# Centring the residual once a step in an AdaLN block of attention and experts

## The reference, cut to what matters

```python
h = layernorm(x) * (1 + ca) + sa
x = x + ga * attention(h)            # 16 heads of 8, window of 32 keys
h = layernorm(x) * (1 + cb) + sb     # this is xt below, 2048 tokens of 128
ew, ei = top_k(xt @ gate_w, 2)       # softmax over the two, spread to wE (experts x tokens)
hid = gelu(xt @ w1[e] + b1[e], approximate=False)        # 256 wide
o = hid @ w2[e] + b2[e]
y = layernorm(xt + o, eps=1e-6) * ln_g[e] + ln_b[e]      # for each of the 8 experts
x = x + gb * sum_e wE[e] * y[e]
```

## Time and profile before

| What | Value |
|---|---|
| Time, median of 3 runs | 253.94 us (253.59 to 254.95) |
| Profiled execution: its own time | 255.15 us |
| Profiled execution: span | 253.4 us |
| TensorE busy / weight loads / VectorE / ScalarE / GpSimd | 91% / 79% / 72% / 61% / 54% |
| Granted TensorE clock, mean | 0.978 |

### The profile page before, as it was taken

How to read it: one execution, slowest core, us unless ns; L and a number is a source line. 1 busy time by engine, 2 the same in 40 slices (tenths; PEclk the granted TensorE clock), 3 DMA queues, 4 the chain that set the end, 5 groups by cost and what they waited for, 6 DMA issues and landing times.

```text
span 253.4 us, 7792 instructions
## 1 busy us (share of the span) xinstructions
PE 230.3 (91%) x3064; PEld 200.6 (79%) x3064; DVE 182.9 (72%) x570; ACT 155.5 (61%) x419; POOL 135.8 (54%) x254
## 2 busy tenths in 40 slices
PE   7976879999899989998999899998999899989960
PEld 3753539988898889887988799888988898869950
DVE  2689957767797859785887689686968596555275
ACT  2165515966498449846695749753984589257740
POOL 8044728246752668247715674366625760378075
PEclk9998879999999999999999999999999999999996
DMA  7940000000000000000000000000000000000000
GB/s 202 360 180 0 3 2 3 0 6 0 4 21 4 3 3 20 4 3 4 0 23 3 0 3 22 5 3 3 21 3 3 3 1 23 4 0 3 21 0 22
DMA packets 5652, 6.23 MB, mean 25 GB/s; under 512 B 336, under 2 KB 5104, under 8 KB 5360
## 3 DMA queue, kind: packets, MB, share of 16 engines
q1 hardware_dynamic: 5616, 5.74, 7.0%
HBM read 4.68 MB, written 1.05 MB: 23 GB/s over the span
## 4 chain that ended last, share of the span: by engine, by line
PE 64%; DVE 25%; POOL 5%; issue 3%; DMA 1%; ACT 1%; POOLq 0%; ACTq 0%; DVEq 0%
PE z L1013 11%; DVE q_st L594 6%; PE score L984 6%; PE score L976 5%; PE turns L871 5%; PE turns L872 4%; PE turns L873 4%; DVE ypart L664 3%; PE score L995 3%; DVE xn L574 3%; PE score L1060 2%; POOL rstd L344 2%; PE turns L1081 1%; PE turns L917 1%; PE turns L1071 1%
## 5 line engine op out<-in xcount | busy, mean ns | idle before, releaser
L1013 PE MATMUL z<-w,hid 128*128 128x128 f32 x480 | 61.6, 276 | 0.0
L1013 PEld LDWEIGHTS z<-w,hid 128*128 128x128 f32 x480 | 58.8, 191 | 3.1 <-issue 1.0
L488 ACT ACTIVATE hid<-turns,pack_ffn 128x256 f32<-128x256 f32 x96 | 38.6, 517 | 32.9 <-PE turns L873 32.9
L327 POOL TENSOR_TENSOR ypart<-ypart 128x256 f32<-128x256 f32 (+1 forms) x60 | 36.1, 601 | 18.4 <-DVE ypart L664 15.4
L313 POOL TENSOR_SCALAR zvar<-zss 128x4 f32<-128x4 f32 x32 | 8.0, 249 | 62.4 <-DVE zss L650 54.4
L664 DVE SCALAR_TENSOR_TENSOR ypart<-z,zcoef,ln_gG 128x128 f32<-128x128 f32 x120 | 34.1, 340 | 1.8 <-POOL zcoef L318 1.7
L314 POOL TENSOR_TENSOR zrstd<-zvar,mhalf 128x4 f32<-128x4 f32 x32 | 32.2, 1008 | 2.7
L871 PE MATMUL turns<-h_hi,w_hi 128*128 128x256 f32 x96 | 27.8, 290 | 0.2 <-DVE h_lo L732 0.2
L872 PE MATMUL turns<-h_lo,w_hi 128*128 128x256 f32 x96 | 27.0, 281 | 0.0
L873 PE MATMUL turns<-h_hi,w_lo 128*128 128x256 f32 x96 | 27.0, 281 | 0.0
L984 PE MATMUL score<-pack_proj,prob 128*128 128x128 f32 x128 | 21.5, 292 | 2.8 <-ACT prob L449 2.8
(11 more groups left out here) (157 smaller groups left out, 517.9 us busy)
## 6 DMA issues: line engine op xcount, KB each, us to landing
w<-in_w SPq DMA_DIRECT2D x2, 1024.0 KB, 8.3
out_x<-yout SPq DMA_DIRECT2D x8, 128.0 KB, 1.8
x_tokens<-in_x SPq DMA_DIRECT2D x1, 896.0 KB, 6.9
ln_g<-in_ln_g SPq DMA_DIRECT2D x1, 512.0 KB
pack_mod<-in_pack_mod SPq DMA_DIRECT2D x1, 385.0 KB, 3.1
pack_proj<-in_pack_proj SPq DMA_DIRECT2D x1, 193.0 KB, 4.2
pack_att<-in_pack_att SPq DMA_DIRECT2D x1, 130.5 KB, 4.1
x_tokens<-in_x SPq DMA_DIRECT2D x1, 128.0 KB, 3.0
```

The costliest lines, as they stand in the source:

```text
L327: cf.link(g.tensor_tensor(ypart[:, tt, at:at + n, :], ypart[:, tt, at:at + n, :], ypart[:, tt, at + n:at + 2 * n, :], ALU.add))
L488: last = a.activation(hid[:, e, c, :], up_bank(i, e)[:, c * STEP:(c + 1) * STEP], ACT.Gelu, bias=b1[:, e, c:c + 1])
L1013: last = mm(z_bank(f, q)[:, e * D:(e + 1) * D], hid[:, ee, c, tt * P:(tt + 1) * P], w2[:, ee * CH + c, :], start=False, stop=e == HALF - 1 ...
```

## The change

Centring moves out of the quarters. `centre(i)`, new on TensorE between up(i,2) and up(i,3), multiplies h2T (fp32, 256 columns) once by a centring matrix whose last output column is zero, so that 127 channels and an empty row come out, into z1 (a score bank in the last step). `split_centred(i)`, new on VectorE between shift(n,1) and shift(n,2), reads that bank, adds a one to row 127 and splits into hc_hi and hc_lo. A quarter is then opened by two matmuls: hc_hi and hc_lo times a `spread_r` matrix that gives back 128 channels from 127 (the last is minus the sum of the others) and whose row 127 holds b2, high part in one copy and low part in the other.

centre(i) waits until scale(f,3) has read z1 (u_done, 4i). down_start(f,0) waits until the split is done (hc_s). In the first part of quarter 1, the products of its first expert move ahead of turn(i,0). On ScalarE the two constant copies (128 x 128 each) give way to one of 128 x 2048; two memsets of ones and one of 128 x 1024 go away on GpSimd; the pack of constants grows by 130 columns.

```diff
@@ scalar front
-                a.activation(ones_r[:, :], ones[:, :], ACT.Copy)
-                a.activation(center_r[:, :], center[:, :], ACT.Copy)
+                a.activation(spread_r[:, :, :, :].rearrange("p a e d -> p (a e) d"), bc(spread[:, :], 1, 2 * EXPERTS),
+                             ACT.Copy).then_inc(spread_s, 1)
@@ vector
+            def split_centred(i):
+                dve.wait_ge(hc_done, i + 1)
+                if i > 0:
+                    dve.wait_ge(z_done, 4 * i)
+                v.tensor_scalar(hc_hi[:, :], hc_bank(i)[:, 0:STEP], units[:, 0:1], None, ALU.add).then_inc(hc_hi_s, 1)
+                dve.wait_ge(hc_hi_s, i + 1)
+                v.scalar_tensor_tensor(hc_lo[:, :], hc_bank(i)[:, 0:STEP], units[:, 1:2], hc_hi[:, :].bitcast(fp32),
+                                       ALU.add, ALU.subtract).then_inc(hc_s, 1)
@@ vector body
-                    for s in range(GROUPS):
-                        shift(n, s)
+                    shift(n, 0)
+                    shift(n, 1)
+                if att:
+                    split_centred(i)
+                if nxt:
+                    shift(n, 2)
+                    shift(n, 3)
@@ tensor down_start
-                mm(by_e, h2_hi[:, f % 2, tok], bc(center_r[:, :], 1, HALF), start=True, stop=False, skip_group_check=True)
-                mm(by_e, h2_lo[:, f % 2, tok], bc(center_r[:, :], 1, HALF), start=False, stop=False, skip_group_check=True)
-                mm(by_e, ones_r[:, :], b2_rows[:, half * HALF:(half + 1) * HALF, :], start=False, stop=False,
-                   skip_group_check=True)
+                experts = slice(half * HALF, (half + 1) * HALF)
+                if q == 0:
+                    pe.wait_ge(hc_s, f + 1)
+                mm(by_e, hc_hi[:, tok], spread_r[:, 0, experts, :], start=True, stop=False, skip_group_check=True)
+                mm(by_e, hc_lo[:, tok], spread_r[:, 1, experts, :], start=False, stop=False, skip_group_check=True)
@@ tensor
+            def centre(i):
+                if i == STEPS - 1:
+                    pe.wait_ge(x1_s, i + 1)
+                elif i > 0:
+                    pe.wait_ge(u_done, 4 * i)
+                mm(hc_bank(i)[:, 0:STEP], center[:, :], h2T[:, :], start=True, stop=True).then_inc(hc_done, 1)
@@ tensor body
                     down_start(f, 1)
+                    products(f, 1, 0, 1)
...
                     up(i, 2)
+                    centre(i)
                     up(i, 3)
```

More of the change, by code:

```diff
@@ L52, in build @@
                  "mask": ((("rep", (P,)), ("masks", (2, KEYS))), P),
-                 "ffn": ((("center", (D,)), ("iota", (EXPERTS,)), ("w_gate", (EXPERTS,)), ("b1", (EXPERTS, CH))), P)}
+                 "ffn": ((("center", (D,)), ("spread", (D,)), ("units", (2,)), ("iota", (EXPERTS,)), ("w_gate", (EXPERTS,)), ("b1", (EXPERTS, CH))), P)}
         packs, part = {}, {}
@@ L69, in build @@
         rep, maskf = part["rep"], part["masks"]
-        center, iota, w_gate, b1 = part["center"], part["iota"], part["w_gate"], part["b1"]
+        center, spread, units, iota, w_gate, b1 = part["center"], part["spread"], part["units"], part["iota"], part["w_gate"], part["b1"]
         b_o = sb("b_o", [P, D])
@@ L78, in build @@
         b2_mean = sb("b2_mean", [EXPERTS, 1])
-        b2_rows = sb("b2_rows", [P, EXPERTS, D], f32r)
+        spread_r = sb("spread_r", [P, 2, EXPERTS, D], f32r)
         b2_high = sb("b2_high", [EXPERTS, D], f32r)
@@ L83, in build @@
         ln_b = sb("ln_b", [EXPERTS, D])
-        center_r = sb("center_r", [P, D], f32r)
         rep16 = sb("rep16", [P, P], bf16)
         mask16 = sb("mask16", [P, 2, KEYS], bf16)
-        ones = sb("ones", [P, P])
         one = sb("one", [P, 1])
@@ L90, in build @@
         table = sb("table", [P, 1])
-        ones_r = sb("ones_r", [P, P], f32r)
         mhalf = sb("mhalf", [P, 8])
@@ L126, in build @@
         h2_lo = sb("h2_lo", [P, 2, STEP], f32r)
+        hc_hi = sb("hc_hi", [P, STEP], f32r)
+        hc_lo = sb("hc_lo", [P, STEP], f32r)
         gsc = sb("gsc", [P, TILES, EXPERTS])
@@ L160, in build @@
         b2_moved = sem("b2_moved")
-        ones_s, pad_s = sem("ones_s"), sem("pad_s")
+        pad_s, spread_s = sem("pad_s"), sem("spread_s")
+        hc_done, hc_hi_s, hc_s = sem("hc_done"), sem("hc_hi_s"), sem("hc_s")
         set_pool, set_act, set_pe = sem("set_pool"), sem("set_act"), sem("set_pe")
@@ L198, in up_bank, with hc_bank @@
             return (U[1], U[0], S[0] if i == STEPS - 1 else zB[0])[e % 3]
+        def hc_bank(i):
+            return S[1] if i == STEPS - 1 else zB[1]
         def here(n):
@@ L255, in _ @@
             sp.wait_ge(set_b2, 1)
-            sp.wait_ge(pad_s, 1)
+            sp.wait_ge(spread_s, 1)
             for row, part_of_b2 in enumerate((b2_high, b2_low)):
-                sp.dma_start(b2_rows[row:row + 1, :, :].bitcast(fp32), part_of_b2[:, :].bitcast(fp32)
+                sp.dma_start(spread_r[P - 1:P, row, :, :].bitcast(fp32), part_of_b2[:, :].bitcast(fp32)
                              ).then_inc(b2_moved, 16)
@@ L272, in _ @@
             g.memset(one[:, :], 1.0)
-            g.memset(ones[:, :], 0.0).then_inc(ones_s, 1)
-            pool.wait_ge(ones_s, 1)
-            g.memset(ones[0:2, :], 1.0)
             g.memset(hT[:, :, 0:BLK], 0.0)
@@ L279, in _ @@
             pool.wait_ge(set_pool, 2)
-            g.memset(b2_rows[:, :, :].bitcast(fp32), 0.0)
             g.memset(ln_bG[:, :, :], 0.0)
@@ L1005, in down, with products @@
             def down(f, q, part, begun=False):
-                half, tt = q // 2, q % 2
                 if part == 0 and not begun:
                     down_start(f, q)
-                for e in range(part * HALF // 2, (part + 1) * HALF // 2):
+                products(f, q, part * HALF // 2 + (1 if begun else 0), (part + 1) * HALF // 2)
+            def products(f, q, first, end):
+                half, tt = q // 2, q % 2
+                for e in range(first, end):
                     ee = half * HALF + e
@@ L1015, in down @@
                                   skip_group_check=True)
-                if part == 1:
+                if end == HALF:
                     last.then_inc(z_done, 1)
@@ L1213 @@
         "iota": np.broadcast_to(np.arange(EXPERTS, dtype=f4), (P, EXPERTS)),
-        "center": (np.eye(D) - 1.0 / D).astype(f4),
+        "center": ((np.eye(D) - 1.0 / D) * (np.arange(D) < D - 1)[None, :]).astype(f4),
+        "spread": ((np.eye(D) - (np.arange(D) == D - 1)[None, :]) * (np.arange(D) < D - 1)[:, None]).astype(f4),
+        "units": (np.arange(D) == D - 1)[:, None].astype(f4) * np.array([[1.0, 2.0]], f4),
         "w_gate": a("ffn_gate_w"), "w1": a("ffn_w1").reshape(EXPERTS, D, CH, P).transpose(1, 0, 2, 3),
@@ L1228 @@
         pack_att=pack(P, "w_v", "headmask", "b_v", "w_o"), pack_mask=pack(P, "rep", "masks"),
-        pack_ffn=pack(P, "center", "iota", "w_gate", "b1"))
+        pack_ffn=pack(P, "center", "spread", "units", "iota", "w_gate", "b1"))
     arrays = {name: np.ascontiguousarray(x) for name, x in arrays.items()}
```

## The result

The changed kernel takes 263.83 us (median of 4 runs, 262.66 to 264.0) against 253.9 (4 runs, 253.59 to 254.95): ratio 1.0355, 95% interval 1.0317 to 1.0392. By the ratio it is 3.6% slower; 262.1 us and 3.2% were forecast. The profiled span goes from 253.4 to 262.1 us.

What follows compares the result with a forecast made beforehand. TensorE (91% busy) bounds only part of a chain shared with VectorE. Body 0 +0.44, bodies 1 to 5 7.15, body 6 +1.22, body 7 -0.47, start -0.20: +8.14 us, to 262.1 us, 3.2% slower; range 257.3 to 265.3.

Steps and rivals of the forecast that it cites:

- The balance of work: TensorE per step: quarters 2 and 3 worth nothing, quarters 0 and 1 -0.46 us, centre +0.45; without any wait, nothing.
- Centre's wait: Centre's weight load among the ups waits 0.78 us for scale(f,3); with 0.45 of work, up(i,3) comes 1.23 us late.
- The split: VectorE's two instructions, 0.48 and 0.47 us with a 0.04 gap; quarter 0 opens 0.21 us later still, 1.44 in all.
- The upper bound of 1.53 us: Most lateness of quarter 0's opening by the bounds of the split's two instructions; the range was 1.32 to 1.53 us.
- No return: From turn(i,0) through probT, square, zsum, xn to turn_x, the lateness stays: 1.43 us per period.
- The 0.99 us of VectorE: The split's added VectorE time ahead of weights(f), claimed hidden because gexp comes later too.
- The start: ScalarE's longer copy delays GpSimd, yet normed_front(1) ends earlier: -0.2 us, or +1.0 if VectorE stays blocked until GpSimd's last.
- Body 7: ... -0.47: Last body: up(7,3) waits for nothing of VectorE's; centre +0.45 and four openings -0.92 give -0.47 us.
- the chain is TensorE's alone: Last body, 232.84 to 242.61 + 1.80: only TensorE sets the pace, the ground for -0.47 us.
- its 263.3: Forecast own time of the profiled execution, from 255.15; 1.2 us above the median, hence 262.1 us forecast.

Runs made afterwards that it cites:

- e5: Kernel before without the third matmul (ones times b2 rows) of each opening, nothing in its place: 254.52 us, ratio 0.9977, period 27.09 us.
- e3: Changed kernel with centre(i) after up(i,3) and split_centred(i) ahead of shift(n,1): 258.48 us, ratio 1.0181, period 27.59 us.
- e4: Changed kernel with the first expert's products of quarter 1 put back behind turn(i,0): 261.96 us, ratio 1.0305, period 28.23 us.
- e8: Kernel before with stats_front moved into the wait for gate, normed_front ahead of weights_T, turn_weights behind turn(i,2): 254.59 us, ratio 0.9998.
- e1: Changed kernel with centre(i) after up(i,3) instead of after up(i,2): 263.09 us, ratio 1.0355, period 28.50 us.
- e2: Changed kernel with split_centred(i) ahead of shift(n,1) instead of behind it: 262.37 us, ratio 1.0322, period 28.23 us.
- e7: e3 plus centre as two f32r matmuls, stats_front into the wait for gate, normed_front ahead of weights_T, turn_weights behind turn(i,2): 255.37 us, ratio 1.0035.

## Why the prediction was right, point by point

**The balance of work.** Quarters 2 and 3 were worth nothing, as predicted: what they saved lengthened the waits of the earlier trace rows by 0.22 and 0.24 us. The prediction counted the other two matmuls as 0.46 us, and so "without any wait" the balance of a step as nothing. That is wrong. In e5 the 0.46 us only lengthened the wait for exp(i,0), and in e3, free of both waits, a period still costs 0.50 us more than before. It did no harm to the sum, because the products moved ahead of turn(i,0) (+0.45) were set against the 0.46.

**Centre's wait.** Predicted 0.78 us for scale(f,3), measured 0.70. Predicted 0.45 us for its work; what is left in e3, free of both waits, is 0.50. That the period came out within 0.02 us (28.52 and 28.50) is in part luck: these two errors are opposite.

**The split.** Predicted 0.48, 0.04 and 0.47 us. The source lines of the changed kernel, with duration in ns as min/median/max:

```profile
L688 DVE TENSOR_SCALAR hc_hi<-z,pack_ffn x7: 473/475/476, 44.7 to 215.5; 128x256 fp32r<-128x256 f32 x7
...
L690 DVE SCALAR_TENSOR_TENSOR hc_lo<-z,pack_ffn,hc_hi x7: 484/485/486, 45.2 to 216.0; 128x256 fp32r<-128x256 f32 x7
```

The wait at the opening was 0.23 us, 0.21 predicted. (The upper bound of 1.53 us leaves out the gap of 0.04 between the two instructions; with it, it is 1.57.) The Trainium skill, "VectorE: DVE Perf Modes", section on the TRN2 errata, would have 0.39 us for each, an estimate for a PSUM source; the rows of the nearest instructions were the better guide.

**No return.** turn(i,0), probT, square, zsum, xn and turn_x were late one after another as predicted, and e4 shows the alternative: with turn(i,0) free to start earlier, 0.27 us of a period return. The 0.99 us of VectorE stayed hidden at weights(f); its slack there is 0.47 us, 0.24 before.

**The start.** normed_front(1) did get in earlier, as the view of the start shows (timeline, after; it answers to the earlier trace rows):

```profile
15.94 1.90 ACT L501 ACTIVATE w_hi<-w 128x2048 fp32r<-128x2048 f32 x1
...
17.92 4.95 POOL L350 TENSOR_TENSOR w_lo<-w,w_hi 128x512 fp32r<-128x512 f32 x4 [1.14 <-ACT w_hi L501]
...
19.34 2.39 DVE L574 TENSOR_SCALAR xn<-x_tokens,mv,rstd 128x128 f32<-128x128 f32 x2
```

GpSimd starts 1.16 us later and xn ends 0.07 earlier, not 1.0 later. The two instructions end within 0.1 us of GpSimd's second and third end (20.42 and 21.64), as the lock of the Trainium skill, "SBUF — State Buffer", section on the two separate sides, has it. The gain is smaller than the 0.20 predicted, as GpSimd began 0.12 later than reckoned.

**The term that was off** is "Body 7: ... -0.47": it measured +0.10. The step that failed is "the chain is TensorE's alone", read as if the end followed TensorE's last matmul. In e5, where only the openings' matmuls are gone, the same stretch is some 0.6 us shorter, not 0.92. In the kernel before, GpSimd's last round of coefficients waits only 0.57 us for the squares of quarter 3 (timeline), so little more than that could be gained before GpSimd's own list decides:

```profile
245.66 0.19 POOL L313 TENSOR_SCALAR zvar<-zss 128x4 f32<-128x4 f32 x1 [0.57 <-ACT zsq L474]
```

In the changed kernel that wait is gone, and the chain at the end leaves TensorE at the last gelu:

```profile
245.95 0.47 ACT hid L488
...
246.44 1.28 ACT L466
...
249.49 0.19 DVE wexp L630
...
249.70 0.65 POOL zrstd L314
...
254.27 1.01 POOL zrstd L314
```

Ahead of that gelu stand centre (+0.45) and only one opening (-0.23). Behind it come the table load, gexp, weights and four rounds of GpSimd's coefficients, of 1.6 us each (the first begins before wexp ends), and these do not get shorter with TensorE's quarters 1 to 3. Counted from the last out_proj, GpSimd's last sum (L335) ends at 28.33 us where it ended at 28.49: 0.16 us less, not 0.47.

The other 0.26 us of the miss stand behind all work. From the end of L335 to the end of the span it is 2.28 us in the kernel before and 2.54 in the changed one. GpSimd's two closing semaphore instructions stand further apart, 0.08 us before and 0.37 now (source line L39, before and then after; first and last start):

```profile
L39 POOLq EVENT_SEMAPHORE  x2: 17/17/17, 253.2 to 253.3; - x2
```

```profile
L39 POOLq EVENT_SEMAPHORE  x2: 17/17/17, 261.6 to 262.0; - x2
```

The seven traces of kernels with the change all have the longer distance, the three without it (before, e5, e8) the shorter. What sets it was not tried.

The spans differ by 8.7 us and the medians by 9.9: the kernel before was profiled in an execution 1.2 us above its median, the changed one in an execution like its median. The prediction took 1.2 us off its 263.3 for that. The profiled execution of the changed kernel took 263.92, so of the 1.7 us between 262.1 and the median of 263.83 only 0.6 are a miss of the sum.

## What to carry to other kernels

Price a removed instruction by the wait that follows it, not by the engine's busy share: here 32 matmuls on the busiest engine (91%) were worth nothing in the steps and 0.6 us in the last body, as each group of them stood ahead of a wait for another engine. A value made once for a whole step has to be ready before the first use; here its producer and its buffer added waits to a stretch that had none. When two waits stand in parallel, remove both before judging either; taken alone, one was worth 0.00 and the other 0.27 us, both together 0.91.

## What the runs showed of the hardware

The start has two lengths. TensorE's first 16 matmul records (silu times w_mod) take 1.84 and 2.05 us in some executions and 1.03 and 1.14 in others, with a granted clock of 1.00 in both; what follows is some 1.6 us earlier or later (mask_q(1) at 29.96 us in the changed kernel, at 28.36 in e1). The short start stands in the traces of e1, e2 and e7, and each of these executions was the fastest of its kernel, by 0.6 to 1.5 us; so it is likely the larger part of the scatter between runs. Timeline, e1 and then the changed kernel:

```profile
4.96 1.03 PE L907 MATMUL score<-silu,pack_mod 128*128 128x2 f32 x8 [0.62 <-DVE silu L751]
5.85 1.14 PE L912 MATMUL z<-pack_mod,silu 128*128 128x128 f32 x8
```

```profile
4.94 1.84 PE L907 MATMUL score<-silu,pack_mod 128*128 128x2 f32 x8 [0.59 <-DVE silu L751]
6.63 2.05 PE L912 MATMUL z<-pack_mod,silu 128*128 128x128 f32 x8
```

What sets it was not tried.

In the profiled execution of e4 a VectorE sum of two columns, 0.15 us elsewhere, lasted 2.81 us while GpSimd multiplied 128 x 1024 elements, and the first opening came over 2 us late:

```profile
41.43 2.81 DVE L711 TENSOR_TENSOR gdif<-gtop 128x2 f32<-128x2 f32 x1
41.81 2.40 POOL L366 TENSOR_TENSOR ln_gG<-ln_g,gates 128x1024 f32<-128x1024 f32 x1
```

A short GpSimd instruction ahead of it (L367) began at 41.40, 0.03 us before VectorE's; in the kernel before the two began at 41.46 and 41.45, and VectorE's took 0.15 us. In all nine other traces VectorE's began level with GpSimd's or up to 0.03 us ahead of it, and took 0.15 us. In e4's it ended at 44.24, 0.03 us behind the long one (44.21). The order of two starts, a few hundredths of a microsecond apart, goes here with 2.7 us; that it is the cause was not tried.
